# An audio tower layer: the attention's inputs from g by a product of two weights, LayerNorm's factor later

## Chip, cores and metric

One core of a Trainium2 chip runs the whole program in one launch. The metric is the device time of an execution in microseconds (us), lower is better. The engines of the core are TensorE (PE; PEld is its weight load), VectorE (DVE), ScalarE (ACT), GpSimd (POOL) and SyncE (SP), which mostly issues DMAs.

## The reference

The input is reshaped to 32 sequences of 94 tokens with 2560 features, 3008 tokens, padded to 24 tiles of 128. Cut to what matters:

```python
x = rms_norm(x, ln_pre_w)                       # 2560 features
h = x @ w1.T                                    # 1024
g = silu(h[..., 512:]) * h[..., :512]           # 512 features per token
y = rms_norm(g @ w2.T, ln_post_w)               # 1024
xn = (y - mean(y)) / sqrt(var(y) + 1e-5)        # LayerNorm
qa = rmsnorm(xn @ wq_a.T)                       # 256
ckv, k_pe = split(xn @ wkv_a.T, 64)             # 64 + 64
ckv = rmsnorm(ckv)
h1 = y + attention(rope(qa @ wq_b.T), ckv @ wkv_b.T, rope(k_pe)) @ wo.T     # 32 heads
out = h1 + lora_moe_linear(layernorm(h1))       # 1024
```

Everything is float32. Products that need the precision are made in three passes over the halves of each operand: a value is split into hi (rounded to fp32r by ScalarE) and lo (the rest, by VectorE), and TensorE adds lo x hi, hi x lo and hi x hi.

## The kernel before

There are five stages, each a block of its own with its own program for each engine: tok_up (up to g, 700 us), tok_down (y, LayerNorm and the attention's inputs, 700 to 1072 us), attention, attn_out and ffn. All weights are resident in a stage. The change is in tok_down.

tok_down runs over 24 tiles of 128 tokens as a software pipeline written out by hand (run_steps, stage): in step s an engine does tile s - D of each part, with D = 0 for the load and split of g, D_Y = 1 for y, D_X = D_A = 3 for the transposes of xn and for a, D_Q = 4 for the transposes of q and k. Each engine does the parts of a step in a fixed order, and counting semaphores hold them together. Six steps are one loop body (U = 6), the first body is written out, and four steps follow the last.

The parts of a tile t:

- SyncE loads g_t (256 KB) and, in step t + 3, the rope table turns (L553), for which it waits for key_done of tile t - 2 (L552, two buffers).
- ScalarE and VectorE split g. TensorE makes ps_y = g w2 by 24 matmuls of 512 columns (L871). There is one ps_y, so y(t) waits for z_done and ysq_done of the tile before (L863).
- VectorE makes z = ps_y * post (L755) and LayerNorm's statistics of z (L757); ScalarE squares ps_y and takes roots (L681, L684, L693); VectorE makes 1/rms and 1/std by two Newton steps; ScalarE writes y (L691), which GpSimd stores (L587); VectorE writes xn, the normalised rows (L778).
- In step t + 3 TensorE turns xn by 8 transposes (L852), ScalarE and VectorE split the result to xt_hi and xt_lo (L647, L732), and TensorE makes ps_a by 24 matmuls of 384 columns (3 passes, 8 blocks of 128 rows of wa, L891).
- ScalarE squares two parts of ps_a and takes the roots (L703 to L708), VectorE scales: qk and kr (L786 to L798). GpSimd applies the rope to kr (L606 to L615, key_done).
- In step t + 4 TensorE transposes qk (L905), and ScalarE and VectorE store qn_hi, qn_lo and k_t, which the attention reads.

Beside this runs work for the attention's weights, 16 folds (one for each pair of heads). A fold has small products wk x wq (fold_q, L829) and wv x wo (fold_v, L837, 512 columns, half of the array's columns at a time). FOLD puts them in steps 2, 3, 5, 6, 8, 9, ...: two steps with a fold, one without. All write ps_f, one after the other: three evictions by ScalarE per fold count f_out up, and the first product of a fold (at the head of its step, ahead of y) waits for the last eviction of the fold before it (L823) and for its weights (L821). SyncE loads those in the fold's own step, behind the turns of that step; the last and largest are two blocks of wo of 512 KB into the ring (L564). GpSimd stores the products. In a step the order on TensorE is: turn xn, fold_q, y (with the other half of fold_q in its middle), fold_v 0, a, fold_v 1, transposes of qk.

At the stage's start SyncE loads g(0), four blocks of w2 (512 KB each), the constants and eight blocks of wa (192 KB each) through a ring of four buffers; ScalarE and VectorE split each block (Splitter, L213, L220).

Of the kernel before, what the change touches and what calls it, by code (L numbers as in the profile page):

```python
# [31 lines left out]
P = 128  # L32
# [7 lines left out]
DM = 1024  # L40
# [380 lines left out]
def tok_down(nc, d, split, ring, ident, qn_hi, qn_lo, k_t):  # L421
# [5 lines left out]
    with ExitStack() as ctx:  # L427
# [3 lines left out]
        wa_hi = mem.sb("wa_hi", [P, KM, W], F32R)  # L431
        wa_lo = mem.sb("wa_lo", [P, KM, W], F32R)
# [3 lines left out]
        g_hi = [mem.sb(f"g_hi{i}", [P, 4, P], F32R) for i in range(2)]  # L436
        g_lo = [mem.sb(f"g_lo{i}", [P, 4, P], F32R) for i in range(2)]
# [9 lines left out]
        xn = [mem.sb(f"xn{i}", [P, DM]) for i in range(2)]  # L447
        xt_hi = mem.sb("xt_hi", [P, KM, P], F32R)
        xt_lo = mem.sb("xt_lo", [P, KM, P], F32R)
# [15 lines left out]
        NW = 4 + KM  # L465
        ws = split.pieces(ring, [d["w2"][:, n, :] for n in range(4)] + [d["wa"][:, n, :] for n in range(KM)])
        ws.into([(w2_hi[:, n, :], w2_lo[:, n, :], None) for n in range(4)] +
                [(wa_hi[:, n, :], wa_lo[:, n, :], None) for n in range(KM)])
        ps_y = mem.ps("ps_y", [P, DM])
        ps_x = [mem.ps(f"ps_x{i}", [P, 4, P]) for i in range(2)]  # L470
# [17 lines left out]
        xn_done = mem.sem("xn_done")  # L488
        x_turned = mem.sem("x_turned")
        xhi_done = mem.sem("xhi_done")  # L490
        xlo_done = mem.sem("xlo_done")
# [22 lines left out]
        D_Y, D_X, D_A, D_Q = 1, 3, 3, 4  # L514
# [19 lines left out]
        def _(sp):  # L534
            def body(k, m):
                s = stage(k, m, 0, U, TILES)
                if s is not None:
                    t, u, kb = s
                    if not first(t, 2):
                        sp.wait_ge(glo_done, t - 1)  # L540
                    sp.dma_start(g_raw[u % 2][:], d["g_t"][t].rearrange("p (j c) -> p j c", j=4)).then_inc(g_in[u % 2], 16)
                    if first(t, 1):
                        for n in range(NW):
                            ws.load(sp, n)
                            if n == Splitter.RING - 1:
                                for dst, name in ((post, "post_ln"), (kvw, "kv_ln"), (qln, "q_ln")):
                                    sp.dma_start(dst[:], d[name]).then_inc(const_in, 16)
# [21 lines left out]
        def _(pool):  # L569
            nc.gpsimd.memset(eps[:], RMS_EPS).then_inc(eps_set, 1)  # L570
            pool.wait_ge(const_in, 48)
# [57 lines left out]
        def _(act):  # L629
            act.wait_ge(eps_set, 1)  # L630

# [7 lines left out]
            def body(k, m):  # L639
                s = stage(k, m, D_X, U, TILES)  # L640
                if s is not None:
                    t, u, kb = s
                    if not first(t, 1):
                        act.wait_ge(a_made, t)
                    for h in range(2):
                        act.wait_ge(x_turned, 2 * t + h + 1)
                        nc.scalar.activation(xt_hi[:, 4 * h:4 * h + 4, :], ps_x[h][:], ACT.Copy).then_inc(xhi_done, 1)  # L647
                s = stage(k, m, 0, U, TILES)
                if s is not None:
                    t, u, kb = s  # L650
                    act.wait_ge(g_in[u % 2], 16 * nth(kb, u))
                    if not first(t, 2):
                        act.wait_ge(y_made, t - 1)
                    nc.scalar.activation(g_hi[u % 2][:], g_raw[u % 2][:], ACT.Copy).then_inc(ghi_done, 1)
                    if first(t, 1):
                        for n in range(NW):
                            ws.split_hi(act, n)
                f = fold(k, m)
                if f is not None:
                    p, b, turn = f  # L660
                    act.wait_ge(f_made, 3 * p + 1)
                    if first(p, 1):
                        act.wait_ge(const_in, 48)
# [7 lines left out]
                if s is not None:  # L671
# [5 lines left out]
                    if not first(t, 2):  # L677
                        act.wait_ge(xn_done, t - 1)
                    act.wait_ge(z_done, t + 1)

                    nc.scalar.activation(junk[:], ps_y[:], ACT.Square, scale=DM ** -0.5,  # L681
# [13 lines left out]
                if s is not None:  # L695
                    t, u, kb = s
                    b = u % 2
                    act.wait_ge(a_made, t + 1)
# [9 lines left out]
                    nc.scalar.activation(root[b][:, 1:3], ms[b][:, 1:3], ACT.Sqrt, bias=eps[:, 0:1]).then_inc(aroot_done, 1)  # L708
# [14 lines left out]
        def _(dve):  # L723
            link = Link(dve, link_sem, 19)

            def body(k, m):
                s = stage(k, m, D_X, U, TILES)
                if s is not None:
                    t, u, kb = s
                    for h in range(2):  # L730
                        dve.wait_ge(xhi_done, 2 * t + h + 1)
                        nc.vector.tensor_tensor(xt_lo[:, 4 * h:4 * h + 4, :], ps_x[h][:], xt_hi[:, 4 * h:4 * h + 4, :],  # L732
                                                ALU.subtract).then_inc(xlo_done, 1)
                s = stage(k, m, 0, U, TILES)
                if s is not None:
                    t, u, kb = s
                    dve.wait_ge(ghi_done, t + 1)
                    nc.vector.tensor_tensor(g_lo[u % 2][:], g_raw[u % 2][:], g_hi[u % 2][:],
                                            ALU.subtract).then_inc(glo_done, 1)
                    if first(t, 1):  # L740
                        for n in range(NW):
                            ws.split_lo(dve, n)
                s = stage(k, m, D_Y, U, TILES)
                if s is not None:
# [4 lines left out]
                    if not first(t, 1):  # L749
                        dve.wait_ge(y_done, t)  # L750
                        dve.wait_ge(xn_done, t)
                    if first(t, 1):
                        dve.wait_ge(const_in, 48)

                    nc.vector.tensor_tensor(z[:], ps_y[:], post[:], ALU.mult).then_inc(z_done, 1)  # L755
# [19 lines left out]
                    link(nc.vector.tensor_tensor(v[:, 7:8], v[:, 7:8], v[:, 1:2], ALU.mult))  # L775
                    if not first(t, 2):
                        dve.wait_ge(x_turned, 2 * t - 2)
                    nc.vector.tensor_scalar(xn[b][:], z[:], v[:, 4:5], v[:, 7:8], ALU.subtract,  # L778
# [1046 lines left out]
```

## Time and profile before

| | us |
|---|---|
| runs: median of 3 (lowest, highest) | 2711.44 (2706.06, 2711.64) |
| profiled execution: span | 2708.5 |
| around the span, by the median | 2.9 |
| TensorE busy | 2569.8 (95%) |
| TensorE weight loads busy | 2242.7 (83%) |
| VectorE busy | 1400.3 (52%) |
| ScalarE busy | 1108.6 (41%) |
| GpSimd busy | 568.0 (21%) |

The profiled execution's own time is known by its span, from its first to its last instruction; the runs' times are taken without the profiler. Busy time is summed over all stages. Matmuls are pipelined and their ends are modelled: a matmul of 512 columns is shown as about 390 ns, while the next one starts much sooner. So distances between starts tell more of TensorE than durations. PEclk is the granted clock of TensorE: 1.00 is 2.4 GHz, 0.50 is 1.2 GHz. Idle time is put down to the engine or DMA that released the instruction.

### The profile page before, as it was taken

What the parts mean: (1) busy time and instruction counts of PE and PEld (TensorE: products, weight loads), DVE (VectorE), ACT (ScalarE), POOL (GpSimd) and SP (SyncE); (2) the same over time, 40 slices, a digit from 0 to 9 for tenths busy, and PEclk for the clock granted to TensorE, in tenths of its full rate; (3) what the DMA queues carried; (4) which work ended last, traced back from release to release, by engine and by line L of the source; (5) the groups of instructions that cost most, each with busy time, mean ns of one, the idle gap of its engine ahead of it and who ended that gap; (6) DMA issues with size and microseconds to landing.
All of it is one profiled execution on the core that took longest, in us unless ns stands there. A gap on an engine that the chain in (4) does not pass through costs nothing. (4 is left out here: it accounts for less than half of the span.)

```text
span 2708.5 us, 47164 instructions
## 1 busy us (share of the span) xinstructions
PE 2569.8 (95%) x15800; PEld 2242.7 (83%) x15800; DVE 1400.3 (52%) x3285; ACT 1108.6 (41%) x3526; POOL 568.0 (21%) x582
## 2 busy tenths in 40 slices
PE   6999999999699997999999999989999999699998
PEld 4888888888577776899999999868888888699998
DVE  5121221222366665799899899841111111777775
ACT  6222222222344444889899899831111110211010
POOL 0000000000011121666666666600000000111110
PEclk9999999999799998999999999989999999899999
DMA  7323233332444543111111111163332222322121
GB/s 238 125 86 127 86 115 98 101 112 89 161 157 153 181 152 114 50 47 42 45 45 41 45 45 41 41 221 102 104 99 93 93 93 70 108 71 71 62 78 47
DMA packets 157346, 260.59 MB, mean 96 GB/s; under 512 B 16432, under 2 KB 92720, under 8 KB 157232
## 3 DMA queue, kind: packets, MB, share of 16 engines
q1 hardware_dynamic: 150048, 233.63, 26.4%
q0 software_dynamic: 7184, 25.69, 2.6%
q8 instruction: 40, 0.66, 0.1%
q14 instruction: 74, 0.61, 0.1%
HBM read 177.49 MB, written 81.79 MB: 96 GB/s over the span
## 5 line engine op out<-in xcount | busy, mean ns | idle before, releaser
L1137 ACT ACTIVATE attn_prob<-attn_prob,attn_bias 94x94 f32<-94x94 f32 x1024 | 367.3, 361 | 58.1 <-DVE attn_bias L1214 58.0
L366 DVE TENSOR_TENSOR up_x_lo<-up_raw,up_x_hi 128x640 fp32r<-128x640 f32 x96 | 79.2, 825 | 474.7 <-ACT up_x_hi L327 474.6
L235 PE MATMUL up_ps_h<-up_w_hi,up_x_lo 128*128 128x512 f32 x960 | 301.5, 396 | 22.1 <-DVE up_w_lo L222 19.1
L235 PE MATMUL up_ps_h<-up_w_lo,up_x_hi 128*128 128x512 f32 x960 | 298.3, 392 | 0.0
L235 PE MATMUL up_ps_h<-up_w_hi,up_x_hi 128*128 128x512 f32 x960 | 298.1, 392 | 0.0
L1346 DVE TENSOR_TENSOR out_x_lo<-out_raw,out_x_hi 128x512 fp32r<-128x512 f32 x96 | 66.5, 693 | 400.0 <-ACT out_x_hi L1331 399.9
L235 PE MATMUL out_ps_h<-out_w_hi,out_x_lo 128*128 128x512 f32 x768 | 238.6, 392 | 11.4 <-DVE out_w_lo L220 10.8
L1331 ACT ACTIVATE out_x_hi<-out_raw 128x512 fp32r<-128x512 f32 x96 | 60.6, 631 | 433.9 <-PE out_ps_h L235 282.7
L1496 POOL TENSOR_TENSOR ffn_res<-shared_h,ffn_bias 128x1024 f32<-128x1024 f32 x24 | 59.7, 2492 | 850.4 <-DMA ffn_bias<-base_b 555.3
L235 PE MATMUL out_ps_h<-out_w_lo,out_x_hi 128*128 128x512 f32 x768 | 237.3, 390 | 0.0
L235 PE MATMUL out_ps_h<-out_w_hi,out_x_hi 128*128 128x512 f32 x768 | 237.2, 390 | 0.0
L1253 POOL TENSOR_TENSOR attn_prob<-attn_prob,attn_share 94x752 f32<-94x752 f32 x128 | 184.3, 1440 | 219.9 <-DVE attn_share L1222 219.9
L235 PEld LDWEIGHTS up_ps_h<-up_w_hi,up_x_lo 128*128 128x128 f32 x960 | 179.0, 189 | 62.1 <-issue 15.7
L235 PEld LDWEIGHTS up_ps_h<-up_w_hi,up_x_hi 128*128 128x128 f32 x960 | 181.5, 189 | 38.6
L235 PEld LDWEIGHTS up_ps_h<-up_w_lo,up_x_hi 128*128 128x128 f32 x960 | 181.4, 189 | 38.4
L327 ACT ACTIVATE up_x_hi<-up_raw 128x640 fp32r<-128x640 f32 x96 | 71.0, 739 | 330.3 <-PE up_ps_h L235 222.5
L1137 ACT ACTIVATION_READ_ACCUMULATOR attn_prob<-attn_prob,attn_bias 94x1 f32 x1024 | 191.6, 187 | 0.0
L235 PEld LDWEIGHTS out_ps_h<-out_w_hi,out_x_lo 128*128 128x128 f32 x768 | 144.0, 188 | 44.1 <-issue 11.3
L235 PEld LDWEIGHTS out_ps_h<-out_w_lo,out_x_hi 128*128 128x128 f32 x768 | 144.8, 188 | 30.2
L235 PEld LDWEIGHTS out_ps_h<-out_w_hi,out_x_hi 128*128 128x128 f32 x768 | 144.5, 188 | 30.0
L235 PE MATMUL ffn_ps_o<-ffn_w_hi,ffn_xt_lo 128*128 128x390 f32 (+1 forms) x576 | 139.8, 351 | 10.2 <-DVE ffn_xt_lo L1584 10.2
L1193 DVE TENSOR_TENSOR attn_prob<-attn_ps_s,attn_mask 94x752 f32<-94x752 f32 x128 | 119.5, 933 | 56.5 <-PE attn_ps_s L1060 56.2
(206 smaller groups left out, 5373.7 us busy)
## 6 DMA issues: line engine op xcount, KB each, us to landing
up_raw<-x_t SPq DMA_DIRECT2D x96, 320.0 KB, 4.4
up_xs<-x_rows SPq DMA_DIRECT2D x96, 320.0 KB, 3.6
out_raw<-o_t SPq DMA_DIRECT2D x96, 256.0 KB, 4.3
o_t<-attn_o_t SPq DMA_DIRECT2D x128, 188.0 KB, 1.9
shared_ring<-wo SPq DMA_DIRECT2D x32, 512.0 KB, 5.2
y<-down_y POOLq DMA_DIRECT2D x24, 512.0 KB, 3.0
out_y<-y SPq DMA_DIRECT2D x24, 512.0 KB, 5.7
h<-out_h SPq DMA_DIRECT2D x24, 512.0 KB, 3.1
```

The source lines that it names most:

```text
L235: last = nc.tensor.matmul(o, x, w, start=a, stop=b, skip_group_check=onto)
L327: nc.scalar.activation(x_hi[c][:], raw[c][:], ACT.Copy).then_inc(hi_done, 1)
L366: nc.vector.tensor_tensor(x_lo[c][:], raw[c][:], x_hi[c][:], ALU.subtract).then_inc(lo_done, 1)
L1137: last = nc.scalar.activation(prob[u % NPR][0:SEQ, h, part], prob[u % NPR][0:SEQ, h, part], ACT.Exp, bias=bias[u % 2][0:SEQ, n:n + 1], sca ...
L1193: nc.vector.tensor_tensor(p4, ps_s[0:SEQ, :, 0:GT].rearrange("p h (b k) -> p h b k", b=GB), mask[0:SEQ, :].unsqueeze(1).unsqueeze(1).broad ...
L1253: nc.gpsimd.tensor_tensor(p4, p4, share[u % 2][0:SEQ, :].unsqueeze(2).broadcast_to((SEQ, 8, SEQ)), ALU.mult).then_inc(prob_done, 1)
L1331: nc.scalar.activation(x_hi[c][:], raw[c][:], ACT.Copy).then_inc(hi_done, 1)
L1346: nc.vector.tensor_tensor(x_lo[c][:], raw[c][:], x_hi[c][:], ALU.subtract).then_inc(lo_done, 1)
L1496: nc.gpsimd.tensor_tensor(res[u % 3][:], h[u % 3][:], bias[:], ALU.add).then_inc(res_done, 1)
```

## The change

LayerNorm's mean is taken out of the weights, and its factor out of the product. With z = (g w2) * post and s the factor 1/(rms std) of a token, xn wa = s (z - mean(z)) wa = s g (w2 diag(post) (wa - column means of wa)). The kernel now makes the folded weight wga = w2 post (wa - mean), 512 x 384, once, and then a = g wga (12 matmuls of 384 columns, straight from g_hi and g_lo) without s. The two roots of a get s^2 as their scale, and s is multiplied in when q, ckv and kr are scaled. xn, its transposes, xt_hi, xt_lo and the split of wa go; y and its LayerNorm statistics stay. ps_y gets two buffers, g_hi and g_lo six. wa lies for the time in k_t's memory.

The diff, cut to its core ("..." marks what is left out):

```diff
-        g_hi = [mem.sb(f"g_hi{i}", [P, 4, P], F32R) for i in range(2)]
+        NG = 6
+        g_hi = [mem.sb(f"g_hi{i}", [P, 4, P], F32R) for i in range(NG)]
...
-        NW = 4 + KM
-        ws = split.pieces(ring, [d["w2"][:, n, :] for n in range(4)] + [d["wa"][:, n, :] for n in range(KM)])
+        NW = 4
+        ws = split.pieces(ring, [d["w2"][:, n, :] for n in range(4)])
-        ps_y = mem.ps("ps_y", [P, DM])
-        ps_x = [mem.ps(f"ps_x{i}", [P, 4, P]) for i in range(2)]
+        ps_y = [mem.ps(f"ps_y{i}", [P, DM]) for i in range(2)]
-        D_Y, D_X, D_A, D_Q = 1, 3, 3, 4
+        D_Y, D_A, D_Q = 1, 3, 4
+        CENTRE_AT = 2
...
         def _(act):
+            act.dma_start(wa, d["wa"]).then_inc(wa_in, 16)
+            for j in range(2):
+                act.dma_start(w2n[j][:], d["w2n"][:, j]).then_inc(w2n_in[j], 16)
+            def spread():
+                act.wait_ge(const_in, 64)
+                for n in range(KM):
+                    act.wait_ge(centred, n + 1)
+                    nc.scalar.activation(wa[:, n, :], wa[:, n, :], ACT.Copy,
+                                         scale=post_col[:, n:n + 1]).then_inc(wp_done, 1)
+            def fold_hi():
+                for j in range(4):
+                    act.wait_ge(wga_made, j + 1)
+                    if j + 2 < 4:
+                        act.dma_start(w2n[j % 2][:], d["w2n"][:, j + 2]).then_inc(w2n_in[j % 2], 16)
+                    nc.scalar.activation(wga_hi[:, j, :], ps_a[j % 2][:, 0:W], ACT.Copy).then_inc(wga_hi_done, 1)
...
-                    if not first(t, 2):
-                        act.wait_ge(y_made, t - 1)
+                    if not first(t, NG):
+                        act.wait_ge(a_made, t - NG + 1)
...
-                    nc.scalar.activation(root[b][:, 1:3], ms[b][:, 1:3], ACT.Sqrt, bias=eps[:, 0:1]).then_inc(aroot_done, 1)
+                    act.wait_ge(norm_done, t + 1)
+                    nc.scalar.activation(root[b][:, 1:3], ms[b][:, 1:3], ACT.Sqrt, bias=eps[:, 0:1],
+                                         scale=norm[u % 3][:, 1:2]).then_inc(aroot_done, 1)
...
+            def centre():
+                dve.wait_ge(mean_made, 1)
+                for n in range(KM):
+                    nc.vector.tensor_tensor(wa[:, n, :], wa[:, n, :], ps_d[:, 0:W], ALU.subtract).then_inc(centred, 1)
+            def fold_lo():
+                for j in range(4):
+                    dve.wait_ge(wga_hi_done, j + 1)
+                    nc.vector.tensor_tensor(wga_lo[:, j, :], ps_a[j % 2][:, 0:W], wga_hi[:, j, :],
+                                            ALU.subtract).then_inc(wga_lo_done, 1)
...
-                    nc.vector.tensor_scalar(xn[b][:], z[:], v[:, 4:5], v[:, 7:8], ALU.subtract,
-                                            ALU.mult).then_inc(xn_done, 1)
+                    nc.vector.tensor_tensor(s3[:, 1:2], s3[:, 0:1], s3[:, 0:1], ALU.mult).then_inc(norm_done, 1)
...
+            def column_means():
+                pe.wait_ge(ones_set, 1)
+                pe.wait_ge(wa_in, 16)
+                for n in range(KM):
+                    last = nc.tensor.matmul(ps_d[:, 0:W], mean_of[:], wa[:, n, :], start=(n == 0), stop=(n == KM - 1))
+                last.then_inc(mean_made, 1)
+            def fold_a():
+                for j in range(4):
+                    pe.wait_ge(w2n_in[j % 2], 16 * (j // 2 + 1))
+                    if j >= 2:
+                        pe.wait_ge(wga_lo_done, j - 1)
+                    for n in range(KM):
+                        if j == 0:
+                            pe.wait_ge(wp_done, n + 1)
+                        last = nc.tensor.matmul(ps_a[j % 2][:, 0:W], w2n[j % 2][:, n, :], wa[:, n, :],
+                                                start=(n == 0), stop=(n == KM - 1))
+                    last.then_inc(wga_made, 1)
...
-                    pe.wait_ge(xn_done, t + 1)
-                            last = nc.tensor.transpose(ps_x[h][:, j, :], xn[u % 2][:, P * n:P * n + P], ident[:])
...
-                    if not first(t, 1):
-                        pe.wait_ge(z_done, t)
-                        pe.wait_ge(ysq_done, t)
+                    if not first(t, 2):
+                        pe.wait_ge(z_done, t - 1)
+                        pe.wait_ge(ysq_done, t - 1)
...
+                    if first(t, 1):
+                        fold_a()
+                        pe.wait_ge(wga_lo_done, 4)
-                    for n in range(KM):
-                        last = three_pass(nc, [ps_a[u % 2][:, 0:W]], xt_hi[:, n, :], xt_lo[:, n, :],
-                                          [wa_hi[:, n, :]], [wa_lo[:, n, :]], n == 0, n == KM - 1)
+                    for n in range(4):
+                        last = three_pass(nc, [ps_a[u % 2][:, 0:W]], g_hi[u][:, n, :], g_lo[u][:, n, :],
+                                          [wga_hi[:, n, :]], [wga_lo[:, n, :]], n == 0, n == 3)
```

column_means and centre run in step 2 (TensorE ahead of y(1), VectorE ahead of z(1)), spread on ScalarE beside them. fold_a runs in step 3, between fold_v 0 and a(0), with fold_hi and fold_lo behind the work of y(2). The matmuls of both are plain fp32 ones.

## Rows read from the trace of the kernel before

**Rows 1.** Grouped lines, 706-1070 us: operation, count; busy us, mean ns; idle before.

```profile
L235 PE MATMUL down_ps_a<-down_wa_hi,down_xt_lo 128*128 128x384 f32 x192 | 67.2, 350 | 4.9 <-DVE down_xt_lo L732 4.9
L235 PE MATMUL down_ps_y<-down_w_hi,down_g_lo 128*128 128x512 f32 x192 | 66.9, 431 | 18.6 <-DVE down_w_lo L220 10.4 <-ACT down_junk L681 8.2
```

**Rows 2.** Waits, 760-1060 us: who for whom; total us, times, longest.

```profile
PE down_ps_f L829 <- DMA shared_ring<-wo: 8.7, 7, 2.0
```

**Rows 3.** Order of time, one period: start us, us, engine, operation, idle before.

```profile
893.27 0.65 PE L829 MATMUL down_ps_f<-down_wk,down_wqn 64*128 64x64 f32 x4 [0.71 <-DMA shared_ring<-wo]
...
907.07 1.04 PE L852 MATMUL down_ps_x<-all_ident,down_xn 128*128 128x128 f32 x8
908.04 0.66 PE L829 MATMUL down_ps_f<-down_wk,down_wqn 64*128 64x64 f32 x4
...
915.25 1.23 DVE L755 TENSOR_TENSOR down_z<-down_ps_y,down_post 128x1024 f32<-128x1024 f32 x1 [4.20 <-PE down_ps_y L235]
...
924.92 0.33 POOL L615 TENSOR_TENSOR down_qk<-down_by_cos,down_by_sin 128x64 f32<-128x64 f32 x1
...
928.48 1.22 DVE L755 TENSOR_TENSOR down_z<-down_ps_y,down_post 128x1024 f32<-128x1024 f32 x1 [2.51 <-PE down_ps_y L235]
...
935.47 0.65 PE L829 MATMUL down_ps_f<-down_wk,down_wqn 64*128 64x64 f32 x4 [1.67 <-DMA shared_ring<-wo]
```

**Rows 4.** Order of time, TensorE: first and last fold waiting for wo.

```profile
765.79 0.66 PE L829 MATMUL down_ps_f<-down_wk,down_wqn 64*128 64x64 f32 x4 [0.64 <-DMA shared_ring<-wo]
...
1020.35 0.65 PE L829 MATMUL down_ps_f<-down_wk,down_wqn 64*128 64x64 f32 x4 [0.47 <-DMA shared_ring<-wo]
```

**Rows 5.** Order of time: a step without fold, then one with it.

```profile
887.03 0.34 PE L235 MATMUL down_ps_a<-down_wa_hi,down_xt_lo 128*128 128x384 f32 x1
...
887.23 1.22 DVE L755 TENSOR_TENSOR down_z<-down_ps_y,down_post 128x1024 f32<-128x1024 f32 x1 [2.09 <-PE down_ps_y L235]
...
891.01 0.34 PE L235 MATMUL down_ps_a<-down_wa_hi,down_xt_hi 128*128 128x384 f32 x1
...
892.88 0.30 ACT L708 ACTIVATE down_root<-down_ms,down_eps 128x2 f32<-128x2 f32 x1
...
895.70 0.21 DVE L798 COPY down_kr<-down_ps_a 128x64 f32<-128x64 f32 x1
...
917.93 0.58 ACT L637 ACTIVATE down_wv_out<-down_ps_f 128x512 f32<-128x512 f32 x1
...
923.63 0.21 DVE L798 COPY down_kr<-down_ps_a 128x64 f32<-128x64 f32 x1
```

**Rows 6.** Order of time, TensorE at the start of y(1).

```profile
724.01 1.19 PE L235 MATMUL down_ps_y<-down_w_hi,down_g_lo 128*128 128x512 f32 x2 [8.22 <-ACT down_junk L681]
```

**Rows 7.** Windows: busy us PE, PEld, DVE, ACT, POOL; PEclk, DMA share, GB/s.

```profile
725.00:730.00 5.00, 5.00 (x14) 3.94 (x13) 3.43 (x14) 2.23 (x5) 1.74 (x2) 0.55 0.89 282
...
852.00:854.00 2.00, 2.00 (x7) 1.53 (x6) 2.00 (x5) 0.00 (x0) 1.58 (x5) 0.60 0.00 0
```

**Rows 8.** Order of time: fp32 matmuls of the fold and of the attention's scores.

```profile
905.68 1.08 PE L837 MATMUL down_ps_f<-shared_ring,down_wv 128*64 128x512 f32 x4
...
1204.05 0.83 PE L1060 MATMUL attn_ps_s<-kept_k_t,attn_q_a 128*94 128x94 f32 x8
1204.71 0.83 PE L1060 MATMUL attn_ps_s<-attn_k_tb,attn_q_b 128*94 128x94 f32 x8
```

**Rows 9.** Order of time, stage start: w2's last split, first fold's end.

```profile
710.78 1.06 ACT L213 ACTIVATE down_w_hi<-shared_ring 128x1024 fp32r<-128x1024 f32 x1 [0.26 <-DMA shared_ring<-w]
...
737.86 1.97 PE L852 MATMUL down_ps_x<-all_ident,down_xn 128*128 128x128 f32 x8
```

**Rows 10.** Windows, the load of w2.

```profile
705.00:710.00 5.00, 2.24 (x5) 1.83 (x6) 1.92 (x2) 2.65 (x3) 0.00 (x0) 0.50 0.97 368
```

**Rows 11.** Order of time, stage end: last z, last transposes of qk.

```profile
1042.37 1.22 DVE L755 TENSOR_TENSOR down_z<-down_ps_y,down_post 128x1024 f32<-128x1024 f32 x1 [4.72 <-PE down_ps_y L235]
...
1070.95 0.87 PE L905 MATMUL down_ps_d<-all_ident,down_qk 128*128 128x128 f32 x3 [4.11 <-POOL down_qk L615]
```

More of the change, by code:

```diff
@@ L430, in tok_down @@
         w2_lo = mem.sb("w2_lo", [P, 4, DM], F32R)
-        wa_hi = mem.sb("wa_hi", [P, KM, W], F32R)
-        wa_lo = mem.sb("wa_lo", [P, KM, W], F32R)
+        assert KM * W == TOKP
+        wa = k_t[:].rearrange("p (n w) -> p n w", n=KM)
+        w2n = [mem.sb(f"w2n{i}", [P, KM, P]) for i in range(2)]
+        wga_hi = mem.sb("wga_hi", [P, 4, W], F32R)
+        wga_lo = mem.sb("wga_lo", [P, 4, W], F32R)
+        mean_of = mem.sb("mean_of", [P, P])
+        post_col = mem.sb("post_col", [P, KM])
         post = mem.sb("post", [P, DM])
@@ L446, in tok_down @@
         y = [mem.sb(f"y{i}", [P, DM]) for i in range(2)]
-        xn = [mem.sb(f"xn{i}", [P, DM]) for i in range(2)]
-        xt_hi = mem.sb("xt_hi", [P, KM, P], F32R)
-        xt_lo = mem.sb("xt_lo", [P, KM, P], F32R)
+        norm = [mem.sb(f"norm{i}", [P, 2]) for i in range(3)]
         qk = [mem.sb(f"qk{i}", [P, W]) for i in range(2)]
@@ L487, in tok_down @@
         yvroot_done = mem.sem("yvroot_done")
[L488 to L491, printed above, removed]
+        norm_done = mem.sem("norm_done")
+        wa_in = mem.sem("wa_in")
+        w2n_in = mem.sems("w2n_in", 2)
+        ones_set = mem.sem("ones_set")
+        mean_made = mem.sem("mean_made")
+        centred = mem.sem("centred")
+        wp_done = mem.sem("wp_done")
+        wga_made = mem.sem("wga_made")
+        wga_hi_done = mem.sem("wga_hi_done")
+        wga_lo_done = mem.sem("wga_lo_done")
         a_made = mem.sem("a_made")
@@ L839, in fold_v @@
                 last.then_inc(f_made, 1)
+            def column_means():
[15 more added lines that the diff above has]
+                    last.then_inc(wga_made, 1)
             def body(k, m):
                 f = fold(k, m)
-                s = stage(k, m, D_X, U, TILES)
-                if s is not None:
-                    t, u, kb = s
-                    pe.wait_ge(xn_done, t + 1)
-                    for h in range(2):
-                        if not first(t, 1):
-                            pe.wait_ge(xlo_done, 2 * t + (h - 1))
-                        for j in range(4):
-                            n = 4 * h + j
-                            last = nc.tensor.transpose(ps_x[h][:, j, :], xn[u % 2][:, P * n:P * n + P], ident[:])
-                        last.then_inc(x_turned, 1)
+                if isinstance(k, int) and k == 0 and m == CENTRE_AT:
+                    column_means()
                 late = f is not None and first(f[0], 1)
@@ L1791 @@
         "post_ln": on_all(L0_tok_ln_post_w),
+        "post_col": np.asarray(L0_tok_ln_post_w).reshape(KM, P).T,
+        "w2n": blocks(np.asarray(L0_tok_w2)).reshape(P, KM, 4, P).transpose(0, 2, 1, 3),
         "wa": blocks(np.concatenate([np.asarray(L0_attn_wq_a).T, np.asarray(L0_attn_wkv_a).T], axis=1)),
```

72 lines of the change are left out of this document (30 added, 42 removed).

## The prediction, made before the changed kernel was run

> **What bounds the kernel now.** I read the page first (TensorE busy 95% of the span, so only stages and waits can tell more), then the grouped lines and the waits of the second stage (tok_down, about 700 to 1072 us), then its order of time. The grouped lines [rows 1] show TensorE's work of a step: 24 matmuls of 512 columns for y, 24 of 384 columns for a (three passes over 8 blocks), and in order of time the 8 transposes of the normalised rows stand ahead of F2's fold [rows 3]. The wait that I take for the key is for a DMA, the load of wo into the ring, 8.7 us in 7 times [rows 2]. Small as it is, it recurs in each period.
>
> The period is three steps. By FOLD, steps 2, 5, 8, ..., 23 and their successors carry a weight fold, every third step none; I call them F1, F2 and N. In [rows 3] the fold of F1 starts at 893.27, that of F2 at 908.04, and the next F1 at 935.47, after a wait for wo. Why is wo late? SyncE issues the loads of step k only behind its turns load, and that waits for key_done of item k-5, which VectorE's step k-2 and then GpSimd make. So the loop is: F1's fold 893.27; F2's fold 908.04 (14.8); z of F2 starts 915.25 (7.2); the key of that step ends 924.92 + 0.33 = 925.25 (10.0); wo is there and F1's fold starts 935.47 (10.2). Sum 42.2. From the first waiting F1 to the last there are six periods: (1020.35 - 765.79) / 6 = 42.43 [rows 4]. Of this 0.5 is the clock (below), so the leg from z of F2 to the next F1 is 42.43 - 0.5 - 14.8 - 7.2 = 19.9. TensorE's work in N lies wholly beside this leg.
>
> **Removed, per step.** Twelve matmuls of a: the 24 of a step without a fold start from 887.03 to 891.01, (891.01 - 887.03) / 23 = 0.173 us apart [rows 5], so 2.07 us. (By columns, one of y is then 0.23, and a y 5.5 us at the full clock.) The 8 transposes stand from 907.07 to 908.04, 0.97 us [rows 3]. So 3.0 us of TensorE per step, 73 us over 24 steps. On the other engines go xt_hi, xt_lo and xn. What is late next:
>
> N: all of the 3.0 us falls on the loop's waiting side. Worth nothing.
>
> F1: TensorE would be at F2's fold 3.0 us earlier, but this fold waits for f_out, ScalarE's last eviction of F1's fold. After the start of z (all offsets from it) the first fold eviction starts at 917.93 - 915.25 = 2.7 and ends at 3.3 [rows 5]; TensorE, through with the short a at about 2.9, waits 0.4 for it. ScalarE's root of a starts 892.88 - 887.23 = 5.65 where it waits for nothing, in fold steps about 5.5; then comes the eviction, behind the root's 0.30 and 0.58 long as the first: over at 6.4, F2's fold at 6.5. Now F2's fold is 14.8 - 7.2 = 7.6 behind z of F1. So 1.1 to 1.2 is gained and not 3.0; F1 to F2 becomes 13.6.
>
> F2 to F1: VectorE's copy of kr starts 895.70 - 887.23 = 8.5 after z, in the F2 step 923.63 - 915.25 = 8.4 [rows 5]. Without xn (0.8) but with the new square (0.2) and dependent scalars it starts at 7.8: 0.6 gained, 19.3 remains. The new waits on norm_done stand three steps behind and cost nothing; with a late norm ScalarE's fold evictions would queue behind it. The two ps_y buffers take away the wait of y for z and the square, which the 5.5 us of y on either side do not need in the loop.
>
> Bare loop: 13.6 + 7.2 + 19.3 = 40.1.
>
> **What the loop gets back.** In F2 TensorE is through 4.75 after z (its fold matmuls from 3.35, 1.0 long, and the transposes of qk). N takes 935.47 - 1.67 - 14.8 - 908.04 = 10.9 now [rows 3], 7.8 then. So it is through with N at 12.6 after z of F2, and wo is there at 19.3: it idles 6.8 us each period instead of the 1.67 of [rows 3]. After an idle of 8.22 us [rows 6] the granted clock was 0.55 for the next 5 us [rows 7], and 5 us at half the rate are 2.5 us lost. Even after a small idle, before 850, the clock fell to 0.60 in 852 to 854 [rows 7]; some 3 us at half the rate are 1.5 lost, and the windows show this in 2 of the 6 periods, the 0.5 above. I bound the cost at 0.5 (as now) and 2.5 (as at 724) and take 2.0, nearer the long idle. Of the Trainium skill, "TensorE: Matmul & The Clock Gate", section "HAM oscillation — how this bites in real kernels", says that a loop which waits on a DMA once per tile can start every tile at the lower clock; by it all periods would pay, which is the upper side, and without it the change would end at the third rival's time. Further, N's y store (512 KB) now starts while wo is still landing (z of N is 10.5 behind z of F2, was 13.2 [rows 3]): between 0 and 1, I take 0.5. The period is then 42.6, 0.2 longer than now; over six periods +1.0, bounds -14 and +10.
>
> **Added at the start.** Forty fp32 matmuls of 384 columns, each two records on TensorE. No row has this shape. Low bound: four of the fold's records of 512 columns take 1.08 together, 0.27 each, so 0.20 for 384 columns, 0.40 a matmul; but these fill half the array's columns each and can overlap in pairs. High bound: 8 records of 94 columns in 1204.71 - 1204.05 = 0.66, 0.083 each, so 0.34 for 384, 0.68 a matmul [rows 8]. I take 0.68, whose output is nearly full width. Fold_a: 32 x 0.68 = 21.8; the column means: 5.4, one more for the low clock at this point.
>
> In order: ScalarE reads w2's last block at 710.78 now [rows 9]. ScalarE's queue sends 2.5 MB (wa, two w2n) beside SyncE's 2.25 MB; at the 368 GB/s of this stretch [rows 10] both end near 715, 4 us later, and y(0) at 719.3. "DMA: Bandwidth & Descriptors", section "Issuing engines are not separate DMA queues" in the Trainium skill, says that loads from several engines share the 16 DMA engines; were they separate, y(0) would be 4 us earlier and so would everything behind it. Then means 6.4 (725.8), y(1) 5.6 (731.4), the first fold 6.0 (737.4; now it ends at 737.86 [rows 9]), F-step up to a 8.1 (745.5), fold_a 21.8 (767.3), its last eviction and subtraction 1.3 (768.6), a(0) 2.1 (770.7), root, scaling and key of item 0 4.5 (775.2), wo 9.2 behind it (10.2 in the loop; fewer transfers stand beside it here): the first waiting F1 starts its fold at 784.4, now 765.79. +18.6. The eight splits of wa that go stood beside y(0) and the load, and only move z(0).
>
> **The end.** F1 to F2 of the last fold pair: 13.6 + 2.0 against 14.8, +0.8. After the last z (1042.37) the last transposes start at 1070.95, 28.6 later [rows 11], since each of the steps 25 to 27 passes turn, split, 24 matmuls, root and key in series. After the change a(22) and a(23) need only g. The rest is the queues' order: key of item 21 at 9.3, its transposes 9.8, a(23) 11.9, root 13.0, kr 14.9, key 16.4: 16.5. So -12.1.
>
> **Sum.** 18.6 + 1.0 + 0.8 - 12.1 = +8.3 on a span of 2708.5: 2716.8. The runs' median, 2711.44, is 2.9 above the span: about 2720 us, +0.3%.
>
> **Rivals.** (1) TensorE's work is the bound, the loads follow. Period 14.8 x 2 + 10.85 - 3 x 3.04 = 31.3, six of them -67, start +14, end -15: 2643. For it: 95% busy. Against: the wait in [rows 2] and that F1's start follows the key by about 10 in the loop. (2) The clock stays high and the store disturbs nothing: -2.3 a period is -14, the start 1 less, the last pair -1.2: 2702, faster. It decides from the point at which an idle of 6.8 us leaves the clock at 1.0; four of the present six waits did, though they were 2 us or less. (3) The fp32 matmuls run at the lower bound: 11 less, 2709, no change to be seen. (4) The clock falls in F2 as well, in which TensorE waits 1.7 before the fold with little work around, and the store costs more: 2.5 more a period, 2735.
>
> **Chances.** Forecast 0.52, (1) 0.05, (2) 0.17, (3) 0.13, (4) 0.13. About 0.2%, 5.4 us, can be told from no change. The forecast, give or take 8, is slower in 0.33, same 0.16, faster 0.03; (1) faster; (2) faster 0.14, same 0.03; (3) faster 0.04, same 0.07, slower 0.02; (4) slower. Faster 0.26, same 0.26, slower 0.48. Range: 2701 (case 2 and the low bounds) to 2735 (case 4); the forecast alone 2712 to 2728.
>
> **What would show it.** After: the period by the starts of F1's folds, 42.6 us, with a wait of 5 to 7 us for shared_ring<-wo before each and the clock low behind it; F2's fold 6.5 after z of F1; fold_a 20 to 23 us long near 745 to 768; the last transposes 16 to 17 after the last z; nothing moved from the third stage on but its start. I am wrong if the waits for wo stay near 1 us (1), if the period is near 40 (2), or if a matmul of fold_a takes under 0.5 us (3).

## The result, and where the time went

The kernel after takes 2773.16 us (median of 4 runs, 2771.51 to 2774.66), the kernel before 2709.67 (4 runs, 2706.06 to 2711.64): ratio 1.0232, 95% interval 1.0219 to 1.0245. The forecast was 2720, its range ended at 2735. The profiled execution took 2774.66 us with a span of 2772.7, 64.2 more than before.

Which part of the span grew can be read from the first matmuls of each stage, kernel before, then kernel after (per tile: duration min/median/max in ns, first and last start in us):

```profile
L1023 PE MATMUL attn_ps_s<-all_ident,kept_k_t x16: 310/312/312, 1076.1 to 1077.7; 64*94 64x64 f32 x16
L235 PE MATMUL out_ps_h<-out_w_hi,out_x_lo x768: 386/390/767, 1773.6 to 2301.2; 128*128 128x512 f32 x192
L235 PE MATMUL ffn_ps_o<-ffn_w_hi,ffn_xt_lo x576: 336/342/695, 2325.7 to 2693.8; 128*128 128x390 f32 x192
```

```profile
L1066 PE MATMUL attn_ps_s<-all_ident,kept_k_t x16: 307/308/308, 1102.5 to 1104.1; 64*94 64x64 f32 x16
L235 PE MATMUL out_ps_h<-out_w_hi,out_x_lo x768: 387/389/762, 1835.9 to 2362.8; 128*128 128x512 f32 x192
L235 PE MATMUL ffn_ps_o<-ffn_w_hi,ffn_xt_lo x576: 336/342/694, 2387.4 to 2757.9; 128*128 128x390 f32 x192
```

The second stage ends 26.4 us later (1102.5 against 1076.1; +8.3 was predicted). The attention stage, of which not one line was changed, takes 733.4 us and not 697.5: +35.9. The out stage takes 551.5 (552.1), the last one 385.3 (382.8). Sum 64.2. So more than half of the loss stands in a stage that the prediction left alone.

**The second stage.** The waits of TensorE, 760 to 1060 us, kernel after, against [rows 2]:

```profile
PE down_ps_f L862 <- DMA shared_ring<-wo: 50.9, 7, 7.9
PE down_ps_f L862 <- ACT down_wv_out L664: 9.3, 6, 1.6
```

The wait for wo grew from 8.7 to 50.9 us, still in 7 times. One period in order of time, kernel after, against [rows 3]; its folds are at L862, z at L786, the last step of the key at L624:

```profile
874.62 1.10 PE L862 MATMUL down_ps_f<-down_wk,down_wqn 64*128 64x64 f32 x4 [7.95 <-DMA shared_ring<-wo]
884.25 1.22 DVE L786 TENSOR_TENSOR down_z<-down_ps_y,down_post 128x1024 f32<-128x1024 f32 x1 [10.99 <-PE down_ps_y L235]
890.73 0.66 PE L862 MATMUL down_ps_f<-down_wk,down_wqn 64*128 64x64 f32 x4 [1.60 <-ACT down_wv_out L664]
898.08 1.22 DVE L786 TENSOR_TENSOR down_z<-down_ps_y,down_post 128x1024 f32<-128x1024 f32 x1 [4.80 <-PE down_ps_y L235]
906.12 0.27 DVE L831 TENSOR_SCALAR down_kr<-down_ps_a,down_norm 128x64 f32<-128x64 f32 x1
907.86 0.32 POOL L624 TENSOR_TENSOR down_qk<-down_by_cos,down_by_sin 128x64 f32<-128x64 f32 x1
918.87 1.10 PE L862 MATMUL down_ps_f<-down_wk,down_wqn 64*128 64x64 f32 x4 [7.87 <-DMA shared_ring<-wo]
```

The ring is as foretold: fold, z, fold, z, key, wo. From the first waiting F1 at 787.46 to the last at 1055.91 there are six periods, 268.45 / 6 = 44.74 us (before 42.43, foretold 42.6). The columns of these windows are those of [rows 7]; the granted clock is at the lower level of 1.2 GHz in the wait for wo and behind F1's fold, and back at 1.0 (2.4 GHz) ten us later:

```profile
874.00:879.00 5.00, 4.38 (x12) 3.60 (x13) 0.00 (x0) 0.00 (x0) 0.90 (x2) 0.50 0.57 175
884.00:894.00 10.00, 8.35 (x40) 5.46 (x39) 7.42 (x27) 5.53 (x15) 2.64 (x6) 1.00 0.21 80
914.00:924.00 10.00, 5.13 (x14) 4.15 (x15) 3.43 (x15) 1.55 (x7) 2.67 (x6) 0.50 0.74 238
```

Start and end of the stage, kernel after (column means L879, folds L862 and L870, weight product L891, last z and last transposes L948), against [rows 9] and [rows 11]:

```profile
719.00 5.32 PE L879 MATMUL down_ps_d<-kept_k_t,down_mean_of 128*128 128x384 f32 x16
729.85 1.37 PE L862 MATMUL down_ps_f<-down_wk,down_wqn 64*128 64x64 f32 x8
733.00 1.90 PE L870 MATMUL down_ps_f<-shared_ring,down_wv 128*64 128x512 f32 x4 [1.78 <-ACT down_wq_out L688]
738.35 1.08 PE L862 MATMUL down_ps_f<-down_wk,down_wqn 64*128 64x64 f32 x4 [0.79 <-ACT down_wv_out L664]
748.74 21.01 PE L891 MATMUL down_ps_a<-kept_k_t,down_w2n 128*128 128x384 f32 x64
787.46 0.90 PE L862 MATMUL down_ps_f<-down_wk,down_wqn 64*128 64x64 f32 x4 [4.96 <-DMA shared_ring<-wo]
...
1079.17 1.23 DVE L786 TENSOR_TENSOR down_z<-down_ps_y,down_post 128x1024 f32<-128x1024 f32 x1 [5.45 <-PE down_ps_y L235]
1097.30 0.87 PE L948 MATMUL down_ps_d<-all_ident,down_qk 128*128 128x128 f32 x3 [4.38 <-POOL down_qk L624]
```

**The attention stage.** TensorE's waits, 1110 to 1830 us, kernel after ("issue" is time in which the engine waited for nothing that the profile shows):

```profile
PE attn_ps_r L1084 <- issue: 24.2, 6, 4.6
PE attn_ps_o L1127 <- DVE attn_o_t L1228: 19.7, 30, 0.9
```

Before, the second of these was 17.7 us in 30 times, and the first did not exist. Six times about 4 us, nobody holds TensorE and it does not work: once at each return from the end of the stage's loop to its start (the loop has seven passes, so six returns). The profile's third part names a queue for this, that of the instructions (packets, MB, share). Before and after:

```profile
q8 instruction: 40, 0.66, 0.1%
```

```profile
q8 instruction: 92, 1.51, 0.2%
```

Between 1300 and 1700 us, inside the attention loop, this queue moves nothing in the kernel before and the following in the kernel after:

```profile
q8 instruction: 39, 0.64, 0.7%
```

That is 39 transfers of 16 KB, nine in a pass of about 90 us. An instruction of the compiled program has 64 bytes, so a transfer holds a block of 256. TensorE's whole program is 10300 instructions before, 40.2 such blocks, and the kernel moves 40: each is loaded about once. After it is 9955 instructions, 38.9 blocks, and 92 transfers. The loop body is 1752 instructions of TensorE, 6.84 blocks, in both kernels. Counted from the first compiled instruction it starts at instruction 4848 before (18 blocks and 240 instructions) and at 4503 after (17 blocks and 151), because the shorter second stage stands ahead of it. My theory A was thus: the loop stays loaded only where it touches few enough blocks, and the change moved it off such a place.

### The profile page after: what moved, and what is told of

It is laid out like the page before. It is cut to its first block and busy times, and to the rows that moved or that the text cites. A ratio compares the mean times of both kernels' runs of the same rounds, so it can differ in the third digit from the quotient of the medians.

```text
span 2772.7 us, 46186 instructions
## 1 busy us (share of the span) xinstructions
PE 2551.8 (92%) x15400; PEld 2206.9 (80%) x15400; DVE 1359.3 (49%) x3241; ACT 1086.2 (39%) x3482; POOL 574.2 (21%) x583
## 5 line engine op out<-in xcount | busy, mean ns | idle before, releaser
L235 PE MATMUL out_ps_h<-out_w_hi,out_x_lo 128*128 128x512 f32 x768 | 238.0, 391 | 11.5 <-DVE out_w_lo L220 11.5
L235 PE MATMUL ffn_ps_o<-ffn_w_hi,ffn_xt_lo 128*128 128x390 f32 (+1 forms) x576 | 139.8, 351 | 10.2 <-DVE ffn_xt_lo L1627 10.2
```

What stands on the lines that cost most here:

```text
L235: last = nc.tensor.matmul(o, x, w, start=a, stop=b, skip_group_check=onto)
```

## The experiments

All "shifted" kernels have more waits on a value long reached ahead of TensorE's first matmul. Two such waits become one instruction, and in the shifted kernels after their number (178, 398 or 458) puts the attention loop back at instruction 240 of its block. The kernel before ran beside each group on the same chip: 2709.74 to 2710.14 us in the three groups.

**Moving the attention loop: after (e1) and before (e2).**

```
             pe.wait_ge(ident_in, 16)
+            for _ in range(178):      # e2: 256
+                pe.wait_ge(ident_in, 16)
```

> The kernel after, with 89 more instructions on TensorE before its first matmul (178 waits on a value long reached, which become 89 instructions), so that the attention stage's loop lies at the same place as before, counted in blocks of 256 instructions. Nothing else. Theory A (the 37.8 us behind the second stage come from TensorE's instructions being loaded again in every pass of the attention loop, and that depends on where the loop lies): attention to out stage back from 733 to about 698 us, the instruction queue back from 1.51 MB to about 0.66 MB, total 2737 (2730 to 2745). Rival B (the attention stage is slower for another reason, its clock or what the changed second stage leaves behind): attention stays at 730 to 736 us, total 2773 within 3.

Measured: 2738.97 us (2735.68 to 2746.21), 1.0109 of before [1.0086, 1.0132]. Against the kernel after that is 34 us less from 89 more instructions.

> The kernel before, with 128 more instructions on TensorE before its first matmul (256 waits on a value long reached), so half a block of 256 instructions later. Nothing else. Theory A: the attention loop is loaded again in every pass, attention from 698 to about 730 us, total 2745 (2735 to 2752), instruction queue near 1.5 MB. Rival B: 2710 to 2715, the price of the added instructions at most.

Measured: 2748.73 (2745.46 to 2753.77), ratio 1.0135 [1.0118, 1.0152]. Instruction queue of e1, then of e2:

```profile
q8 instruction: 39, 0.64, 0.1%
```

```profile
q8 instruction: 94, 1.54, 0.3%
```

Start of the attention and of the out stage in e1, then TensorE's waits in e2's attention, 1085 to 1810 us:

```profile
L1068 PE MATMUL attn_ps_s<-all_ident,kept_k_t x16: 311/311/312, 1103.4 to 1105.0; 64*94 64x64 f32 x16
L235 PE MATMUL out_ps_h<-out_w_hi,out_x_lo x768: 388/389/765, 1799.5 to 2327.1; 128*128 128x512 f32 x192
```

```profile
PE attn_ps_r L1043 <- issue: 23.8, 6, 4.2
```

e1's attention takes 1799.5 - 1103.4 = 696.1 us, with the second stage as in the kernel after (start 1103.4 against 1102.5). e2's takes 735.1 in a kernel that holds nothing of the change. Theory A holds and rival B is out. The six waits are 24.2 us in the kernel after; behind them the granted clock is at 0.50 for 3 to 7 us each, 27.5 us in all, which at half the rate costs at most 13.7 us more (an estimate). Together they cover the 35.9 us.

**Is it the place within a block (e5), and is it the number of blocks (e6)?** e5 is the kernel before with 512 of these waits, one whole block. e6 is the kernel before with a longer loop, started at the same place within a block:

```
                     pe.wait_ge(rope_b_done, j + 1)
+                    for _ in range(8):
+                        pe.wait_ge(v_done, 4)
```

> The kernel before with 256 more instructions on TensorE before its first matmul: one whole block, so that the attention loop lies as before within its blocks. If the place within a block of 256 instructions (16 KB, the size of one transfer of the instruction queue) decides: attention 696 to 698 us, instruction queue near 0.66 MB, total 2710 to 2718 (the added instructions themselves may cost up to 8 us at the start). If any shift of the code does it, or the added instructions cost the time: 2745 or more.

Measured: 2715.06 (2707.23 to 2718.83), ratio 1.0018 [1.0007, 1.003]; instruction queue 41 transfers, attention 695.9 us. One block further nothing is loaded again; half a block further (e2) the loop is, at every return.

> The kernel before with 63 more instructions in one pass of TensorE's attention loop (128 waits on a value long reached, 1752 to 1815 instructions), its start at the same place within a block as before. 1815 instructions are 7.09 blocks of 256 and can't lie within 7; 1752 are 6.84 and can. If the loop must lie within 7 blocks to stay loaded: attention near 730 to 745 us, instruction queue near 1.5 MB, total 2745 to 2760. If the length has no such limit: attention up by what the instructions themselves cost, under 10 us, total under 2722.

Measured: 2746.02 (2744.6 to 2750.61), ratio 1.0136 [1.0116, 1.0156]; attention 735.7 us, TensorE's waits there, 1085 to 1810 us:

```profile
PE attn_ps_r L1043 <- issue: 25.2, 6, 4.5
```

95 transfers of instructions (94 in e2). (The added instructions are 64 a pass, 1816 in all, not 63 and 1815; 7.09 blocks either way.) A loop that grew from 6.84 to 7.09 blocks costs the same as one that was shifted by half a block. So what counts is how many blocks the loop touches, seven or more than seven. The transfers bear this out: a kernel that loads each block once moves one for each border that it passes. In the first pass of the loop, the kernel before (1165 to 1248 us), then the kernel after (1190 to 1273 us) move:

```profile
q8 instruction: 6, 0.10, 0.5%
```

```profile
q8 instruction: 7, 0.11, 0.6%
```

Six borders are seven blocks touched, seven are eight. e1 has 6 in its first pass, e2 and e6 have 7, and in the kernel before no further transfer comes until the loop is left, at 1751 us. The place that counts is not a block of the compiled program counted from its first instruction: by that count (240 of block 18 to 199 of block 25, or 151 of block 17 to 110 of block 24) the loop would touch eight in both kernels. The borders of the transfers lie elsewhere; for six in the one and seven in the other they must lie between 200 and 240 of 256 in that count (an estimate). Seven blocks are 1792 instructions, 40 more than the loop has, so only 41 of the 256 possible places keep it loaded, and the kernel before happened to lie in one of them. The Trainium skill, "Runtime: NRT & Kernel Launch", section "Instruction fetch mechanics", gives blocks of 16 KiB and 128 KiB of instruction memory for TensorE, eight blocks, with the next one loaded ahead, and warns of taken branches whose target is not there; with 16 KB a transfer and a limit at seven blocks of loop plus one ahead the runs agree. The same section speaks of two lines of 16 KiB, and of a window of two blocks outside which a taken branch has to load its target first; by that the loop of the kernel before would be loaded again at each return, and here the measurement decides: its trace has no transfer between 1249 and 1747 us.

**The ring through wo: the fold's loads first, after (e3) and before (e4).** In SyncE's body the block of the fold moves ahead of the block of the turns:

```
+                s = fold(k, m)          # loads of wq_nope, wk, wq_rope, wv, wo
+                ...
                 s = stage(k, m, D_A, U, TILES)
                 if s is not None:
                     t, u, kb = s
                     if not first(t, 2):
                         sp.wait_ge(key_done, t - 1)
                     sp.dma_start(turns[u % 2][:], d["turns"][t])...
-                s = fold(k, m)
-                ...
```

> As the shifted kernel after, and SyncE issues the loads of the fold (wq_nope, wk, wq_rope, wv, wo) ahead of the load of the turns, which waits for the key of two tokens' tiles ago. Loop theory (the period is a ring: key, then wo's load, then the first fold, z, second fold, z, key): the 7 waits for wo of about 7.3 us go, the period falls from 44.7 to 33 to 37 us, the second stage by 50 to 75 us, total 2665 to 2690. Rival (another chain stands close behind: TensorE or VectorE at 40 us or more a period): period 40 or more, total 2705 or more.

Measured: 2673.72 (2668.81 to 2675.69), ratio 0.9856 [0.9838, 0.9875]. It beats both kernels. Order of time, one period of e3 (folds at L864, z at L788):

```profile
889.07 0.66 PE L864 MATMUL down_ps_f<-down_wk,down_wqn 64*128 64x64 f32 x4
896.33 1.23 DVE L788 TENSOR_TENSOR down_z<-down_ps_y,down_post 128x1024 f32<-128x1024 f32 x1 [0.31 <-PE down_ps_y L235]
902.74 0.66 PE L864 MATMUL down_ps_f<-down_wk,down_wqn 64*128 64x64 f32 x4 [1.53 <-ACT down_wv_out L666]
910.00 1.23 DVE L788 TENSOR_TENSOR down_z<-down_ps_y,down_post 128x1024 f32<-128x1024 f32 x1 [4.78 <-PE down_ps_y L235]
922.83 0.66 PE L864 MATMUL down_ps_f<-down_wk,down_wqn 64*128 64x64 f32 x4
```

No wait for wo is left and the period is 922.83 - 889.07 = 33.8 us. TensorE is the bound, but for the 1.5 us before F2's fold.

> The kernel before with the same order of loads on SyncE. Before, the wait for wo was 0.7 to 1.7 us in six of its folds and once 8.7, so the ring and TensorE's own work lay close together: period from 42.4 to about 40.5, total 2698 (2690 to 2708). If the ring through wo's load was the only bound, then lower: 2680 or less; if it was none, 2709.

Measured: 2696.23 (2693.68 to 2701.91), ratio 0.9952 [0.9934, 0.9969]. Folds of one period of e4:

```profile
882.42 0.66 PE L829 MATMUL down_ps_f<-down_wk,down_wqn 64*128 64x64 f32 x4
897.19 0.66 PE L829 MATMUL down_ps_f<-down_wk,down_wqn 64*128 64x64 f32 x4
922.88 0.66 PE L829 MATMUL down_ps_f<-down_wk,down_wqn 64*128 64x64 f32 x4
```

Period 40.5. (The expectation misreads [rows 2]: 8.7 us is the sum of the seven waits, the longest is 2.0.) With wo out of the ring in both and the loop well placed, the change takes the kernel from 2696.23 to 2673.72: 22.5 us less, and 6.7 a period. Its gain was there; the ring hid it.

**The clock term (e7).** TensorE is kept at work in the wait for wo, in every F1 step but the stage's first:

```
                 if h == 0:
+                    if b == 0 and not first(p, 2):
+                        pe.wait_ge(f_out, 3 * p)
+                        for i in range(24):
+                            nc.tensor.matmul(ps_f[:], w2_hi[:, 0, 0:P], w2_hi[:, 0, 0:512], start=True, stop=True)
                     pe.wait_ge(fold_in[b], 96 * turn + 96)
```

> The shifted kernel after, with 24 matmuls of 512 columns (about 5.4 us) into the fold's free psum ahead of each wait for wo but the first, so that TensorE idles 2 us there and not 7.5; their result isn't used. Clock theory (the low clock behind the long idle costs 2.0 to 2.5 us a period): from F1's fold to z 7.2 us, not 9.6; granted clock not near 0.5 behind the fold; period 44.7 to about 42.4; total 2738.97 less 14 to 17, 2722 to 2725. Rival (the fall doesn't come from the idle, or the period is bound by something the clock doesn't touch): 2737 to 2741.

Measured: 2727.46 (2726.64 to 2731.45), ratio 1.0069 [1.0051, 1.0088], 11.5 us less than e1. Folds of F1 in e7, then windows of e7:

```profile
871.21 0.66 PE L868 MATMUL down_ps_f<-down_wk,down_wqn 64*128 64x64 f32 x4 [1.64 <-DMA shared_ring<-wo]
912.79 0.66 PE L868 MATMUL down_ps_f<-down_wk,down_wqn 64*128 64x64 f32 x4 [2.08 <-DMA shared_ring<-wo]
957.23 0.66 PE L868 MATMUL down_ps_f<-down_wk,down_wqn 64*128 64x64 f32 x4 [2.09 <-DMA shared_ring<-wo]
```

```profile
871.00:876.00 5.00, 4.79 (x23) 3.75 (x24) 0.00 (x0) 0.43 (x2) 1.20 (x4) 1.00 0.36 99
...
957.00:962.00 5.00, 4.78 (x16) 3.56 (x16) 0.00 (x0) 0.00 (x0) 0.77 (x2) 0.70 0.52 143
...
972.00:977.00 5.00, 4.52 (x14) 3.71 (x15) 2.85 (x12) 1.39 (x4) 3.05 (x8) 0.66 0.41 159
```

The first three periods, 788.38 to 912.79, are 41.5 us each, at the full clock. The last three, to 1045.70, are 44.3 us: the granted clock is 0.70 behind F1's fold at 957.23 and 0.66 behind F2's at 972.48, though the waits are as short. So the low clock costs about 44.74 - 41.47 = 3.3 us a period in the kernel after, 3.1 of it in the two legs from a fold to z, and a wait of 2 us doesn't rule it out. The clock theory is right in kind; 2.0 to 2.5 was too small for it, and the filling cured it half the time.

**The start (e8, e10).** e8: one block of 8 in the means and the product. e10: besides, w2n isn't loaded again for the third and fourth product, and centring and scaling are done for one block.

```
-                    for n in range(KM):
-                        if j == 0:
-                            pe.wait_ge(wp_done, n + 1)
+                    if j == 0:
+                        pe.wait_ge(wp_done, KM)
+                    for n in range(1):
                         last = nc.tensor.matmul(ps_a[j % 2][:, 0:W], w2n[j % 2][:, n, :], wa[:, n, :], ...
```

> The shifted kernel after with one eighth of the weight product: one block of 128 rows in place of 8 in the column means and in each of the four products (the rest of the sum is left out). Start theory (these fp32 matmuls stand on the path that sets when the loop begins): 7/8 of 21.0 and of 5.3 us go, so the first waiting fold comes 23 us earlier and the total is 2716 (2713 to 2720). Rival (the start is set by the loads of wa, w2n and w2, which stay): first waiting fold 10 us earlier or less, 2729 or more.

Measured: 2732.25 (2730.53 to 2734.24), ratio 1.0083 [1.0065, 1.0101]: 6.7 us less than e1, not 23; the first waiting fold moved from 788.76 to 781.05. TensorE's waits in e8, 700 to 1100 us, show what stood behind the product:

```profile
PE down_ps_a L893 <- DMA down_w2n<-w2n: 6.7, 1, 6.7
...
PE down_ps_f L872 <- ACT down_wq_out L690: 6.3, 1, 6.3
```

ScalarE issues the loads of the third and fourth part of w2n only when the first two products are made, and ScalarE's eviction of the first fold waits behind the scaling. My start theory counted the product as if nothing stood beside it; it fell. A third thing took back part of the 23 us: with its long work gone TensorE waits, and the granted clock is 0.50 from 755 to 768 us, where e1 has 1.00 from 748 to 768. At half the rate that is at most 6.5 us (an estimate).

> As the shifted kernel after with one eighth of the weight product, and with its covers taken away too: the third and fourth product use the first two blocks of w2 again instead of waiting for a new load (6.7 us in the run before), and the centring on VectorE and the scaling on ScalarE are done for one block of 8 instead of 8, so that ScalarE's eviction of the first fold isn't late (6.3 us in the run before). Seven eighths of the product, of the centring and of the scaling are left out, and w2's second half. Theory (behind the product stood two covers of 6.7 and 4.5 us, the scaling and the reload): first waiting fold at 781.05 less 11, 770; total 2720 to 2723. Rival (the start is set by the loads and the low clock there): first waiting fold at 777 or later, total 2727 or more.

Measured: 2723.77 (2719.57 to 2724.74), ratio 1.0041 [1.0027, 1.0055], first waiting fold in e10:

```profile
773.60 0.66 PE L860 MATMUL down_ps_f<-down_wk,down_wqn 64*128 64x64 f32 x4 [3.83 <-DMA shared_ring<-wo]
```

Seven eighths of means, product, centring and scaling, and the reload, are worth 15.2 us of the start, and 7.8 us over the kernel before (765.79) remain for what still stands ahead, among it the 2.5 MB that ScalarE's queue loads beside SyncE's, and the clock, 0.51 from 751 to 761 us; which part costs what was not tried. The first fold lies midway between the two theories' 770 and 777, the total nearer the first.

**The store beside wo (e9).** GpSimd puts off the store of y of an N step to behind the wait for wo:

```
-                s1 = stage(k, m, D_Y, U, TILES)
-                if s1 is not None:
+                for back in ((1, 0) if m % 3 == 2 else () if m % 3 == 1 else (0,)):
+                    s1 = stage(k, m - back, D_Y, U, TILES)
+                    if s1 is not None:
```

> The shifted kernel after, with GpSimd's store of y in the steps without a fold (512 KB, issued while wo is landing) put off to the next step, behind the wait for wo. Contention theory (this store delays wo): from the end of the key to the first fold 10.7 falls to about 9.9, the period from 44.7 to about 44.0, total 3 to 6 us below 2738.97. Rival (wo lands behind the other loads and stores whatever this one does): 10.5 or more from the key to the fold, total within 2 us. Where the stores collide with the second fold's work instead, ScalarE waits for y_stored and the total rises.

Measured: 2736.5 (2733.48 to 2741.0), ratio 1.0099 [1.0082, 1.0116], which overlaps e1's. In the profiles the distance from the key's end to F1's fold falls from 10.2 (mean of six in e1) to 9.7, the period from 44.6 to 44.3. The 0.5 us of the prediction is seen in the trace. The total can't tell it: e9's first waiting fold also comes 5.1 us earlier than e1's (783.69 against 788.76), where the granted clock from 734 to 744 us is 1.00 in e9 and 0.51 in e1.

## Why the prediction was wrong

**The step that failed** is "nothing moved from the third stage on but its start". I took a stage whose code is the same as costing the same. It cost 35.9 us more, and e1, e2, e5 and e6 show why: the place of TensorE's attention loop among the instruction blocks, which any edit ahead of it moves. The profile of before held the number to look at: the instruction queue moved only 40 transfers in all for a program of 40.2 blocks, so that a loop of 6.84 blocks must have stayed loaded. Taken alone, with this repaired, the change gives 2738.97, still 3.97 us above the range's end: the second stage too was priced too low, at +8.3 and not +26.4.

**The loop: +1.0 foretold, +13.9 measured.** Means over the six periods: F1's fold to z 9.65 (foretold 7.2 + 2.0), z to F2's fold 6.42 (6.4, as foretold to 0.1), F2's fold to z 8.07 (7.2), z to the end of the key 10.05 (9.4), key to F1's fold 10.55 (10.4 with the store). Of the 2.1 us too few, 1.3 lie in the two legs from a fold to z, and are the clock: against e7's periods at the full clock (7.27 and 7.32) it costs 3.1 us there and not 2.0, 2.4 in F1 in every period and 0.75 on average in F2, where it fell in two of six, which was rival 4. All seven waiting F1 folds started at the low clock (their four matmuls take 0.90 to 1.11 us, at the full clock 0.66). The Trainium skill, "TensorE: Matmul & The Clock Gate", section "HAM oscillation — how this bites in real kernels", says that a loop which waits on a DMA once per tile can start every tile at the lower clock; for these waits of 5 to 8 us the trace agrees. Another 0.5 lies in GpSimd: from the start of VectorE's kr to the end of the key 1.62 us before, now 2.06 in three of the periods and 2.23 in the other three. In the three the rotation's two products with the sine last 0.93 us from start to end and not 0.49, in the others the product with the cosine 0.88 and not 0.32. Order of time of GpSimd, before and after:

```profile
924.35 0.49 POOL L610 TENSOR_TENSOR down_by_sin<-down_kr,down_turns 128x32 f32<-128x32 f32 x2
```

```profile
906.85 0.93 POOL L619 TENSOR_TENSOR down_by_sin<-down_kr,down_turns 128x32 f32<-128x32 f32 x2
950.46 0.88 POOL L615 TENSOR_TENSOR down_by_cos<-down_kr,down_turns 128x64 f32<-128x64 f32 x1 [1.44 <-DVE down_kr L831]
```

Each of the long ones runs beside VectorE's subtraction for g_lo (L768, from 906.64 and from 950.48), which before started at 925.29, behind the start of the key's last product. The last four steps of the kernel after have no g_lo left, and in them all are as short as before. That this is the cause was not tried by itself. The rest is VectorE's kr, 0.1 later on average than worked out (8.04 or 7.75 behind z for 7.8).

**The start: +18.6 foretold, +21.7 measured.** The fp32 matmuls were right: 21.01 / 32 = 0.66 us each, 0.68 was taken, so rival 3 is out. Means over at 724.3 (725.8 foretold), but the first fold took 8.5 us up to the next (729.85 to 738.35) and not 6.0, with 1.8 us of waiting for ScalarE, which was scaling wa, and its matmuls at the low clock; the next step took 10.4 up to the product and not 8.1, with the granted clock at 0.51 from 733 to 743. That e8 gave back only 7.7 us of 23 shows that the foretold sum, though near in size, was a sum over one path where two more stood close behind it, and the clock with them.

**The end: -12.1 foretold, -10.5 measured** (last z to last transposes 18.1, before 28.6; 16.5 was foretold), and the last pair of folds to the last z +1.2 for +0.8: a part of the last products of a ran at the low clock.

**The rivals.** (1) was right on what would be left without the ring: e3's period is 33.8 where it had 31.3; its condition, that the loads follow, wasn't met. (2) is out, the clock fell each time. (4), a period of 45.1, is nearest to the 44.74 measured; its 2735 is 4.0 below e1, of which the start's 3.1 too few are the larger part. None of them, and not the range, had a term for code that does not change.

## What to carry to other kernels

Before an edit that shortens or lengthens an engine's program, look at the instruction queue in the profile: if it moves nothing during a long loop, the loop is resident, and its length in 256-instruction blocks says how near it is to losing that (here 6.84 blocks with seven as the limit: at most 40 instructions to spare, 36 us at stake). Compare stages whose code is the same first; if one of them has changed, shift the program so that its loop starts at the same place within a block as before, and measure again before judging the edit. And when a loop waits on a load that is issued behind a wait for the loop's own result, take the load out of the ring first: here the saving of work was seen only after that (22.5 us).

## What the runs showed of the hardware that I had not expected

TensorE's attention loop made its stage 36 to 40 us longer where it didn't stay loaded (733.4, 735.1 and 735.7 us; 695.8 to 697.5 in the other nine kernels): six waits of about 4 us, one at each return to the loop's start, and behind each of the six the granted clock fell to 0.5 for 3 to 7 us, which no profile with a resident loop shows in that stretch. The same kernel is 1.35% slower or not by 128 instructions that do nothing. Of where exactly the borders lie the runs give three points, with start at 240 of 256 (resident), 151 and 112 (not); the points between were not tried. The clock did not follow the length of the wait alone: in e7 waits for wo of 2.22, 1.64 and 1.72 us left it high, while within 2 us behind those of 2.08, 2.09 and 1.87 us it fell to the low level. And wherever VectorE's subtraction for g_lo ran beside GpSimd's small products, in each step of the kernel after from 788 to 1055 us, they took about 0.45 or 0.55 us longer.
